# Two-layer graph kernel on one Trainium2 core: dense groups started inside the last block, and destination halves of 14 attention tiles made ahead

## The reference, cut to what matters

```python
# x: 12500 x 256; src, dst: 200000 edges, sorted by dst
def layer0(Z, U, Dmat, head_w):            # K = 4 heads of R = 16
    ZU = einsum('nd,kdr->knr', Z, U)
    logits = (ZU[:, src] * ZU[:, dst]).sum(-1) / sqrt(16)
    alpha = segment_softmax(logits, dst)
    agg = segment_sum(alpha * ZU[:, src], dst)      # 12500 x 64
    Z_half = 0.5 * Z + 0.5 * einsum('k,knr,kdr->nd', softmax(head_w), agg, U)
    return relu(Z_half + 0.5 * ((Z_half - Z_half @ Dmat.T @ Dmat) @ Dmat) - 0.05)
def layer1(x, weight, attn_l, attn_r):     # heads 4 of 64
    xt = (x @ weight).reshape(-1, 4, 64)
    a = softmax(leaky_relu(xt[src].attn_l + xt[dst].attn_r), over heads)   # first 12500 edges only
    return repeat4(einsum('nh,nhd->nd', a[:n], xt[dst[:n]]))
x = layernorm(x + layer0(x)); out = layernorm(x + layer1(x))
```

## Time and profile before

| | |
|---|---|
| three runs, us | 2481.39, 2479.98, 2479.67 (median 2479.98) |
| the profiled execution, us | 2478.89 |
| its span (first to last instruction), us | 2476.7 |
| mean granted TensorE clock | 0.623 |
| busy share PE / DVE / ACT / POOL | 74% / 77% / 47% / 70% |
| last scan of the blocks ends at, us from the span's start | 2121.93 |
| first dense matmul, last dense matmul | 2130.11, 2228.84 |
| first source fetch | 2241.04 |

### The profile page before, as it was taken

How to read it: one execution, slowest core, us unless ns; L and a number is a source line. 1 busy time by engine, 2 the same in 40 slices (tenths; PEclk the granted TensorE clock), 3 DMA queues, 4 the chain that set the end, 5 groups by cost and what they waited for, 6 DMA issues and landing times.

```text
span 2476.7 us, 61813 instructions
## 1 busy us (share of the span) xinstructions
PE 1835.3 (74%) x15251; PEld 1434.1 (58%) x15252; DVE 1912.4 (77%) x5864; ACT 1157.1 (47%) x3040; POOL 1742.5 (70%) x1832
## 2 busy tenths in 40 slices
PE   9576777767777777677777677777776776896885
PEld 9355555555555556555555555555555555556775
DVE  6676877868778788687777787778777787894888
ACT  2124453544534435444354453444534444466887
POOL 2777777777777777777777777777777773556772
PEclk9555555655555565555655555555565555898997
DMA  9223323233233333333233232332333323894553
GB/s 305 65 54 71 76 61 73 64 67 75 62 70 66 71 72 64 69 67 69 62 73 70 64 72 65 70 69 63 73 69 66 69 63 101 287 332 131 164 164 112
DMA packets 406593, 232.96 MB, mean 94 GB/s; under 512 B 284096, under 2 KB 371434, under 8 KB 406506
## 3 DMA queue, kind: packets, MB, share of 16 engines
q1 hardware_dynamic: 346666, 154.11, 22.6%
q0 software_dynamic: 59840, 77.87, 14.6%
HBM read 134.80 MB, written 42.55 MB: 72 GB/s over the span
## 4 chain that ended last, share of the span: by engine, by line
POOL 34%; issue 23%; DMA 14%; PE 11%; SPq 9%; ACT 3%; DVE 3%; POOLq 2%; ACTq 0%; DVEq 0%
POOL arena L582 34%; DMA arena<-z_table,sslot 14%; SPq L437 8%; PE bank L1508 2%; PE bank L1478 2%; PE bank L1250 2%; POOLq L579 2%; ACT arena L1667 2%; PE bank L1482 1%; ACT L1700 1%; PE bank L1498 1%; PE bank L1510 1%; PE bank L1272 1%; SPq L431 0%; PE bank L1456 0%
## 5 line engine op out<-in xcount | busy, mean ns | idle before, releaser
L582 POOL DMA_INDIRECT arena<-z_table,sslot x1563 | 1508.0, 965 | 529.0 <-issue 447.5
L1353 PE MATMUL bank<-arena 128*128 x4992 | 558.8, 220 | 124.7 <-DVE xin L908 82.7
L1590 ACT ACTIVATE arena<-bank 128x272 f32<-128x272 f32 x416 | 274.6, 661 | 769.9 <-PE bank L1370 756.6
L1353 PEld LDWEIGHTS bank<-arena 128*128 128x128 bf16 x4992 | 444.6, 104 | 248.4 <-issue 146.8
L908 DVE TENSOR_TENSOR xin<-arena,bank 128x512 f32<-128x512 f32 x208 | 143.0, 688 | 393.5 <-DMA arena<-arena 256.6
L1567 ACT ACTIVATE acc<-xTb 128x68 f32 x1600 | 361.1, 311 | 9.2 <-ACT acc L1567 0.5
L1370 PE MATMUL bank<-arena 128*128 128x68 bf16 x1664 | 294.1, 245 | 78.2 <-DVE xto L1042 77.8
L1341 PE MATMUL bank<-ident_b,arena 128*128 128x128 bf16 x1664 | 214.8, 310 | 132.1 <-DVE arena L899 118.5
L1370 PE MATMUL bank<-xto,arena 128*128 128x68 bf16 x3328 | 309.7, 248 | 0.0
L899 DVE TENSOR_SCALAR arena<-iota_b,didx 128x128 bf16<-128x128 bf16 x1664 | 300.8, 275 | 6.5
L1370 PEld LDWEIGHTS bank<-xto,arena 128*128 128x128 bf16 x3328 | 281.5, 133 | 0.0
(11 more groups left out here) (264 smaller groups left out, 2539.6 us busy)
## 6 DMA issues: line engine op xcount, KB each, us to landing
arena<-arena SPq DMA_DIRECT2D x1660, 32.0 KB
arena<-z_table,sslot POOLq DMA_INDIRECT x1563
dspace<-in_xT SPq DMA_DIRECT2D x49, 256.0 KB
xmz_table<-agn SPq DMA_DIRECT2D x49, 256.0 KB
xmz_table<-arena SPq DMA_DIRECT2D x14, 896.0 KB, 8.9
arena<-in_x SPq DMA_DIRECT2D x13, 896.0 KB, 11.2
out<-arena SPq DMA_DIRECT2D x12, 896.0 KB, 4.7
xin<-in_xT SPq DMA_DIRECT2D x8, 896.0 KB, 8.3
```

The lines of the kernel that those rows point to most:

```text
L582: pool.indirect_dma_start(ring[:, e % RING, :], None, z_table, bass.IndirectOffsetOnAxis(ap=sslot[:, e:e + 1], axis=0)).then_inc(tiles_in[ ...
L1353: last = T.matmul(zd_ps[g % 2][:, u * KR:(u + 1) * KR], onehotT[:, g * G + u, :], z3[:, bass.ds(tiles[u], 1), s, :].rearrange("p a c -> p ...
L1590: A.activation(sums[:, :, 1 + q * Q:1 + (q + 1) * Q].rearrange("p c j -> p j c"), sum_ps[q % 2][:, 0:Q * AW].rearrange("p (j c) -> p j c", ...
```

## The change

In the blocks' end: DVE takes the reciprocals of tiles 0 to 13 before the last scan, and those of the other 84 tiles inside its dense loop, before the step of tile 3. POOL scales groups 0 and 1 before it stores its states of the last scan. PE transposes group 0 right after its last block into banks 4 and 5 and multiplies tiles 0 to 3; then come 32 dummy matmuls, the wait for the last scan, and group 1's transposes. The 96 dummy matmuls of before are gone.

In the attention stage: 14 tiles (`EARLY`) have their destination halves transposed and multiplied as soon as the dense stage is over, with the copies on DVE. When their source rows come, PE transposes 2 blocks and multiplies 4 columns, ACT copies half a tile and 4 columns, and DVE adds the two scores. POOL fetches 12 more destination tiles (`REFILL`) into slots that the early transposes have freed, before it turns to the source fetches. SP's program is unchanged.

```diff
+EARLY = 2 * T7
+REFILL = 2 * DW
```

On POOL:

```diff
+            pool.wait_ge(rec_ready, 1)
+            for g in range(2):
+                scale_sums(g)
             tiles = last_tiles(mybir.EngineType.Pool, 3)
             pool.wait_ge(scan_done, NB)
...
-            for g in range(NG7):
-                pool.wait_ge(rec_ready, 1 if g < 2 else 2)
+            for g in range(2, NG7):
+                pool.wait_ge(rec_ready, 2)
+                scale_sums(g)
...
+            for n in range(DRING, DRING + REFILL):
+                if n % DW == 0:
+                    pool.wait_ge(rows_stored, pool.value_load(dneed[0:1, n + DW - 1:n + DW], min_val=1, max_val=NG7))
+                    nc.gpsimd.nop(nofuse=True)
+
+                pool.wait_ge(gT_ps, n - DRING + 1)
+                fetch_dst(n)
+
             pool.wait_ge(rows_stored, NG7)
-            fetched = DRING
+            fetched = DRING + REFILL
             for n in range(NT):
                 h, t = n // T7 % 2, n % T7
                 if n >= 2 * T7:
-                    pool.wait_ge(gT_ps, n - 2 * T7 + 1)
+                    pool.wait_ge(gT_ps, EARLY + n - 2 * T7 + 1)
...
-                while n >= 2 * T7 and fetched < DRING + share:
+                while n >= 2 * T7 and fetched < DRING + REFILL + share and fetched - DRING <= max(EARLY - 1, n - 2 * T7):
```

On DVE (`reciprocals(t0, t1)` holds the two instructions of before for those tiles):

```diff
+            dve.wait_ge(xmz_out, 16 * NY)
+            dve.wait_ge(state_stored, B * (NB - 2))
+            reciprocals(0, 2 * T7)
             begin_scan(NB - 1)
...
             for k in range(NT + 6):
+                if k == YB - 1:
+                    reciprocals(2 * T7, NT)
...
-                dve.wait_ge(xt1_copied, n1)
+                dve.wait_ge(xt1_copied, EARLY + n1)
+                if n1 <= EARLY:
+                    V.tensor_tensor(xto[:, h, 0:m, HO:XW], xto[:, h, 0:m, HO:XW], xto[:, h, 0:m, XW:WW], ALU.add).then_inc(v_step, 1)
+                    dve.wait_ge(v_step, vn.next())
...
+            for i in range(EARLY + GB - 1):
+                if i < EARLY:
+                    dve.wait_ge(gT_ps, i + 1)
+                    if i >= GB:
+                        dve.wait_ge(xt1_ps, i - GB + 1)
+                    V.tensor_copy(gT[i % GB][:, DC * P:2 * DC * P], gT_bank[i % GB][:, DC * P:2 * DC * P]).then_inc(gT_ready, 1)
+                if i >= GB - 1:
+                    n = i - GB + 1
+                    dve.wait_ge(xt1_ps, n + 1)
+                    V.tensor_copy(xto[:, n // T7, n % T7, 0:XW], psum[2 + n % YB][:, 0:XW]).then_inc(xt1_copied, 1)
```

On PE (`transpose_rows(i, n, src, dst)` and `project_rows(i, src, dst)` now take which halves they do; i counts transposed tiles over both passes; bank 4 and 5 take the transposes of group 0):

```diff
-            pe.wait_ge(scan_done, NB)
-            keep_busy(WARM)
-            pe.wait_ge(rec_ready, 1)
-            keep_busy(WARM // 4)
             transpose_sums(0)
-            keep_busy(WARM // 4)
...
-                if t == (1 if g == 0 else 0) and g < NG7 - 1:
+                if n == YB - 1:
+                    keep_busy(WARM // 2)
+                    pe.wait_ge(scan_done, NB)
+                    transpose_sums(1)
+                elif t == 0 and 1 <= g < NG7 - 1:
                     transpose_sums(g + 1)
...
+            for i in range(EARLY + GB - 1):
+                if i < EARLY:
+                    transpose_rows(i, i, False, True)
+                if i == GB - 1:
+                    pe.wait_ge(y_added, NT)
+                if i >= GB - 1:
+                    project_rows(i - GB + 1, False, True)
             for n in range(NT + GB - 1):
                 if n < NT:
-                    transpose_rows(n)
+                    transpose_rows(EARLY + n, n, True, n >= EARLY)
+                if n == GB - 1:
+                    pe.wait_ge(xt1_copied, EARLY)
                 if n >= GB - 1:
-                    project_rows(n - GB + 1)
+                    project_rows(EARLY + n - GB + 1, True, n - GB + 1 >= EARLY)
```

On ACT (its copies in the attention stage are as wide as the half in question: 256 and 4 columns for the first 14 tiles):

```diff
+            copy_sums_T(0)
             tiles = last_tiles(mybir.EngineType.Activation, 0)
...
-            copy_sums_T(0)
+            act.wait_ge(last_stored[1], STORES)
+            act.wait_ge(last_stored[2], 2 * STORES)
             copy_sums_T(1)
```

100 lines of the change are left out of this document (58 added, 42 removed).

## The result

The changed kernel took 2486.91 us (median of ten runs, 2483.98 to 2504.22) against 2476.54 us of the kernel before in the same sessions: ratio 1.0056, 95% interval 1.0042 to 1.0070. It is slower by more than the 0.2% that the prediction took as the bound. In microseconds the forecast was +2.8 (2482.8 against 2479.98), and the measured difference is +10.4. The profiled execution took 2484.66 us, with a span of 2482.8 us and a mean granted clock of 0.620 (before 2478.89, 2476.7 and 0.623).

What follows compares the result with a forecast made beforehand. PE was taken to set the dense stage's pace, with DVE and the DMA engines hardly behind. Dense end +1.3 and attention +1.5 on the profiled 2478.9 gave 2481.7 us (2482.8 against the median), range 2473 to 2487.5.

Steps and rivals of the forecast that it cites:

- the blocks stay as they are: Blocks before the last scan: claimed untouched, so only the final 355 us could move.
- the clock's term: PE behind the wait for group 4's products: half clock on resuming costs 2.2 us, bounds nothing and 2.5.
- the 5.0 us of the bound: Whole kernel: a difference of 0.2% (5.0 us) is about what a measurement can tell from no change.
- Group 4's products: Dense stage: PE comes 5.3 us earlier but waits 4.3 us for this load; only 0.9 us slack is gained.
- Attention part, +1.5: Attention stage: group 0's logits 1.1 us later because refills delay source fetches, +1.5 us at group 1, then unchanged.
- the stated bands: Behind the last dense matmul: first source fetch at 15 to 19 us, group 0's logits at 31 to 35 us.
- never held PE there: Attention stage: POOL has 12 fetches fewer among the source fetches, 15 us less work, but never held PE.
- Rival 1: Group 4's load does not hold PE: the dense part gives its 5.3 us, time 2476.2; chance 12%.
- rival 3: No clock lost at either wait: dense -0.9, attention near 0, time 2479.1; chance 15%.
- rival 5: The change does not do what it says; no size given; chance 3%.
- Rival 2: Dense and attention parts both give their full gains, -5.3 and -4.4 us, time 2470.3; chance 8%.
- Rival 4: Clock stays at 0.5 through PE's early destination work in the attention stage: +9 us, time 2489; chance 12%.

Runs made afterwards that it cites:

- h3: Dense part of the change alone (`p1`) with 48 dummy matmuls in PE's wait for group 4's products: 2481.83 us, ratio 1.0004 to the kernel before.
- b3: Dense part alone (`p1`) with 64 dummy matmuls behind PE's last work, giving PE's program its old length: 2487.58 us, ratio 1.0053 to the kernel before.
- c1: The changed kernel, unchanged, run and profiled once more: 2488.58 us, ratio 1.0052 to the kernel before.
- p1: Only the dense part of the change, added to the kernel before, attention stage as before: 2486.83 us, ratio 1.0060 to the kernel before.
- k3: The changed kernel, unchanged, run once more on the chip of `k1`: 2497.26 us, ratio 1.0079 to the kernel before.
- k1: The changed kernel with group 4's products loaded earlier, no refills, and the two early scalings on DVE instead of POOL: 2473.71 us, ratio 0.9981 to the kernel before.
- g1: Only the attention part of the change, added to the kernel before, with REFILL at 0: 2474.34 us, ratio 0.9996 to the kernel before.
- g2: The changed kernel with group 4's products loaded earlier and REFILL at 0, early scalings still on POOL: 2475.11 us, ratio 0.9996 to the kernel before.
- f1: Dense part alone (`p1`) with the loads of group 4's and 5's products issued earlier in SP's queue: 2476.59 us, ratio 1.0001 to the kernel before.

## Why the prediction was wrong

The forecast was no measurable change, by a sum of +2.8 us, and the kernel became 10.4 us slower. That 2486.91 still lies between the stated 2473 and 2487.5 is luck: the prediction counted from 2479.98, the median of three runs, and the median of all ten was 3.4 us lower. Two steps failed, that the blocks stay as they are and the size of the clock's term.

- **"The change leaves the blocks alone, so all that can move lies after the last scan."** This step failed. The blocks became some 4 us slower, by POOL's early scalings (6.5 in the first pair of profiles, 2.8 of them ahead of the first gather), and that alone would have used up the 5.0 us of the bound. No row of the profile of before told it, and no rival had it.
- **Group 4's products.** Right in place and cause, and the slack of 0.9 us was 0.8. PE came less early than forecast: I had it 5.3 us ahead. It was 2.9 ahead at group 2's transposes (rel 23.5 against 26.4). Its dummies ran at half clock (32 in 3.59 us, where `h3` has 48 in 2.85), as did the transposes of groups 0 and 1 (1.67 and 1.37 us for seven, 0.93 at full clock), and DVE's scan began 0.55 us later behind the reciprocals (rel 4.90 against 4.35). Both had been costed at nothing. So the wait was 1.49 to 2.79 us in the five profiles that have it, not 4.3. That did not matter for the sum, since only the slack counts.
- **"I take 2.2, near the row"** for the low clock: the mis-sized term. The row it came from, 3.47 us of idle time and 5 us at 0.50, was one case of something that varies. Behind waits of 1.49, 1.88, 1.93, 2.71 and 2.79 us (the changed kernel first, `b3`, `c1`, `p1`, `k3`) the clock stayed low for 3.4, 17.1, 17.1, 17.1 and 30.7 us, and the dense end came at rel 116.5, 122.5, 122.7, 122.5 and 128.9, that is 0.5 to 12.9 us later than before, where I had +1.3. By `h3` the clock costs 7.4 us where it stays low for 17. What sets how long it stays low, no run shows. I bounded the term by "nothing" and "2.5 by this row"; one row is no upper bound. The sentence of the Trainium skill (TensorE: Matmul & The Clock Gate, Part 1), that the cost of the slow start is under 1% of a typical span, holds as a share here: 7.4 of 2480 us is 0.3%. It was still larger than every other term of the sum.
- **Attention part, +1.5.** Measured alone: tail +1.7 (366.2 against 364.5), median +0.9. The path was nearly as told: PE's pause of 3.85 us with half clock behind it, the refills with waits for PE, the first source fetch 17.7 us behind the end of the dense matmuls and the logits of group 0 33.6 behind it, both inside the stated bands. In the part alone they are 19.0 (the edge of the band) and 36.2 (1.2 above it). The size is partly luck, since the start lost more than the 1.1 I had: 4.3 us at group 0. Of these, 0.7 was won back by the third group and 1.6 at the twelfth (rel 316.3, before 314.4), for a reason that was not tested. That POOL "never held PE there" held with hardly any margin: before, PE began tile 90 at 2431.21, 4.4 us behind the destination fetch of tile 95, which in `k1` took 4.5 us to land. So in `g1`, whose groups ran up to 5.4 us earlier with POOL's fetches mixed as before, PE stands for POOL there.
- **The rivals.** Rival 1 (the load doesn't hold PE) and rival 3 (no clock lost) are refuted in all profiles of the change, rival 5 too. Rival 2 (2470.3) is refuted by the time; even with both waits mended the tail is 5.4 to 5.7 us shorter (`k1`, `g2`), not 9.7. Rival 4 had the right sign, the right mechanism and by chance nearly the time (2489), but the wrong place: the clock stayed low behind group 4. In the early destination work it was back at 1.00 after 3.4 to 6.8 us.
- **The sum with measured terms**, first session's kernels: dense start without the wait -2.7 (tail of `f1`), the wait and the clock behind it +8.2 (`p1` against `f1`), attention +1.7, blocks +4.3: +11.5. Measured: 2488.58 - 2476.55 = 12.0 (10.4 in the ten first runs). That it comes so near is partly luck: the terms are from single profiles, and the tail of the changed kernel itself was 364.1, 372.4 and 376.2 in its three.

## What to carry to other kernels

Where a change brings an engine earlier to a load whose issue is fixed by a queue, move the load in the same edit. If it can't be moved, fill the wait with dummy work, because the clock behind the wait can cost several times the wait (here, in one pair of profiles, 7.4 us against 2.6). Compare each stage by medians of runs with one part of the change alone: a stage whose code is untouched can change its time, and one profile can't tell that from scatter.
